# Host-transposed weights and a GpSimd time mix in a two-layer attention, expert and RWKV kernel

## The reference

```python
# first layer, experts
shared = silu(x @ sg_w.T) * (x @ su_w.T) @ sd_w.T
h = silu(einsum('th,eih->eti', x, eg_w)) * einsum('th,eih->eti', x, eu_w)
routed = einsum('eti,ehi,te->th', h, ed_w, comb)          # comb: routing factors
# second layer, each of 4 RWKV layers l
hx = time_shift(h)                                        # the token before
r = sigmoid((h * tmr + hx * (1 - tmr)) @ Wr.T)            # the receptance; k and v alike
x = x + (r * wkv(decay, first, k, v)) @ Wo.T
k2 = square(relu((h2 * cmk + hx2 * (1 - cmk)) @ Wck.T))
x = x + sigmoid((h2 * cmr + hx2 * (1 - cmr)) @ Wcr.T) * (k2 @ Wcv.T)
```

## Time and profile before

| | us |
|---|---|
| median of 3 runs | 1093.31 |
| lowest, highest | 1084.61, 1096.35 |
| the profiled execution | 1086.78 |
| its span (first to last instruction) | 1084.8 |
| PE busy in the span | 1020.1 (94%) |
| DVE busy | 768.1 (71%) |
| ACT busy | 582.5 (54%) |
| GpSimd busy | 63.6 (6%) |
| mean granted TensorE clock | 0.985 |

### The profile page before, as it was taken

The page is one execution under the profiler, slowest core; times in us unless marked ns, Lnnn a source line. Parts: engine busy times, 40 slices in busy tenths (PEclk is TensorE's granted clock), DMA queues, the critical chain, the costliest instruction groups (busy, mean ns, idle before and its releaser), DMA issues. The chain is left out here.

```text
span 1084.8 us, 12618 instructions
## 1 busy us (share of the span) xinstructions
PE 1020.1 (94%) x3858; PEld 445.8 (41%) x3858; DVE 768.1 (71%) x1332; ACT 582.5 (54%) x902; POOL 63.6 (6%) x152
## 2 busy tenths in 40 slices
PE   6889999999889999999999999879999999998998
PEld 3553444443333444444444443324344443443433
DVE  4879888888467555555555555588889988987575
ACT  4235666667774222222222222668789778875743
POOL 1011222222110000000000000000000000000000
PEclk9899999999999999999999999989999999999999
DMA  3732121200142544555545461100000020000001
GB/s 96 231 83 51 38 47 45 55 26 11 30 103 45 122 106 102 128 114 116 124 106 129 101 136 41 42 0 23 10 21 12 1 51 1 0 1 1 0 1 39
DMA packets 49980, 64.68 MB, mean 60 GB/s; under 512 B 17570, under 2 KB 41232, under 8 KB 45328
## 3 DMA queue, kind: packets, MB, share of 16 engines
q1 hardware_dynamic: 49100, 63.28, 25.1%
q10 hardware_dynamic: 832, 0.79, 0.2%
HBM read 55.87 MB, written 5.77 MB: 57 GB/s over the span
## 5 line engine op out<-in xcount | busy, mean ns | idle before, releaser
L977 ACT ACTIVATE pt<-psum 128x1024 f32<-128x1024 f32 (+1 forms) x192 | 150.2, 815 | 106.0 <-PE psum L748 105.6
L1131 DVE TENSOR_REDUCE part_max<-psum 128x1 f32<-128x512 f32 (+3 forms) x304 | 184.2, 658 | 31.9 <-PE psum L730 19.3
L1288 DVE TENSOR_TENSOR moe_gu<-moe_silu,psum 128x512 f32<-128x512 f32 x132 | 90.8, 688 | 150.4 <-PE psum L891 146.1
L1115 ACT ACTIVATE moe_silu<-psum 128x512 f32<-128x512 f32 x112 | 66.9, 598 | 200.0 <-PE psum L886 200.0
L891 PE MATMUL psum<-h,moe_wt 128*128 128x512 f32 x264 | 135.3, 594 | 1.5 <-DVE moe_gu L1288 1.5
L886 PE MATMUL psum<-h,moe_wt 128*128 128x512 f32 x264 | 134.9, 593 | 1.0 <-issue 1.0
L896 PE MATMUL psum<-moe_hid,moe_wt 128*128 128x512 f32 x264 | 135.0, 593 | 0.7 <-DVE moe_hid L1296 0.7
L726 PE MATMUL psum<-ka,qa 72*128 72x512 bf16 (+3 forms) x384 | 113.6, 337 | 4.5 <-DVE part_max L1131 1.6
L748 PE MATMUL psum<-qa,ka 75*128 75x512 bf16 (+3 forms) x384 | 93.8, 326 | 2.6 <-DMA qa<-neg_t 1.6
L1296 DVE TENSOR_TENSOR moe_hid<-moe_gu,qa 128x512 f32<-128x512 f32 x120 | 83.1, 692 | 13.6 <-DVE moe_gu L1288 5.8
L764 PE MATMUL psum<-pt,va_g 128*32 128x512 f32 (+3 forms) x768 | 81.8, 498 | 0.5 <-POOL pt L697 0.3
(11 more groups left out here) (274 smaller groups left out, 1362.3 us busy)
## 6 DMA issues: line engine op xcount, KB each, us to landing
qa<-comb_rows SPq DMA_DIRECT2D x56, 512.0 KB, 6.2
qa<-rows_q SPq DMA_DIRECT2D x21, 192.0 KB
ka<-rows_k SPq DMA_DIRECT2D x21, 192.0 KB
o_den<-acc SPq DMA_DIRECT2D x32, 64.0 KB, 2.1
moe_raw<-in_L_ffn_eg_w SPq DMA_DIRECT2D x32, 64.0 KB, 5.5
moe_raw<-in_L_ffn_eu_w SPq DMA_DIRECT2D x32, 64.0 KB, 5.3
moe_raw<-in_L_ffn_ed_w SPq DMA_DIRECT2D x32, 64.0 KB, 5.0
qa<-comb_rows SPq DMA_DIRECT2D x16, 128.0 KB, 3.2
```

Of the source, the lines that this page charges most:

```text
L977: act.activation(pt[:, u % 4, :, 0:n], score_bank[u % 2][:, :, 0:n], ACT.Exp, scale=SCALE)\
L1115: act.activation(sg[:, c % 2, :], g_bank[:, :], ACT.Silu).then_inc(silu_done, 1)
L1131: dve.tensor_reduce(part_max[:, h0:h0 + heads, slot], bank_of("fill", f)[:, 0:heads * nk].rearrange("p (h n) -> p h n", h=heads), AX_X, AL ...
L1288: dve.tensor_tensor(gu[:, at % 2, :], sg[:, at % 2, :], u_bank[:, :], ALU.mult).then_inc(gu_done, 1)
```

## The change

The host lays out three arrays, `moe_w`, `time_w` and `channel_w`, with the contraction dimension first. Then:

- The raw tiles of the expert weights, all `turn_weights` and `keep_weights` are gone. Loads go straight into the tiles that PE reads. The first five sets are loaded in one go during attention; after that, gate and up weights of step s + 2 are loaded into the tile of step s once its last `up` is done (`u_psum`), and the down weight once its last `down` is done (`y_psum`).
- In the RWKV stage `turn_a`, `turn_c` and `keep_c` are gone; the channel weights have two tiles by turns; the output weight is loaded in place; `keep_a` makes four scaled copies and one plain copy from SBUF in place of seven operations from PSUM.
- GpSimd makes `mix_r` = (here - before) * tmr + before, in three operations of 128x512 for each half unit, 48 in all. PE does one receptance product on it in place of two. `channel_scale` of DVE waits for GpSimd's mixing of the same unit, one body earlier.

```diff
-def load_experts(sp, G, A, s, k):
-    ...
+def load_expert(sp, A, s, tile, what, sem):
+
+    sp.dma_start(tile[:, what, :], A["moe_w"][bass.ds(s, 1), :, what, :].rearrange("o p j m -> p (o j) m")).then_inc(sem, 16)
...
                 with sp.Fori(PRE // 2, (STEPS - 3) // 2) as i:
                     for k in (1, 0):
                         s = 2 * i + 2 - k
-                        sp.wait_ge(w_turned, s + 1)
-                        load_experts(sp, G, A, s + 2, k)
+                        sp.wait_ge(u_psum, 4 * s + 4)
+                        load_expert(sp, A, s + 2, wt[k], slice(0, 2), gu_in[k])
                         sp.wait_ge(hid_done, 4 * s + 4)
                         factors(s + 2, factor[1 - k], slice(0, T), factor_in[1 - k])
+                        sp.wait_ge(y_psum, 4 * s + 4)
+                        load_expert(sp, A, s + 2, wt[k], slice(2, 3), down_in[k])
...
-                        if c == 1 and not last:
-                            turn_weights(s + 1, 1 - k)
+                        if c == 2:
+                            pe.wait_ge(down_in[k], 16 * loads)
...
+                for u in range(UNITS):
+                    for q in range(2):
+                        n = 2 * u + q
+                        pool.wait_ge(h_time, n + 1)
+                        if u:
+                            pool.wait_ge(r_psum, n - 1)
+                        pool.tensor_tensor(mix_r[:, q, :], here(u, q), before(u, q), ALU.subtract).then_inc(mix_step, 1)
+                        pool.wait_ge(mix_step, 2 * n + 1)
+                        pool.tensor_scalar(mix_r[:, q, :], mix_r[:, q, :], vec(TMK + 2, u), None, ALU.mult).then_inc(mix_step, 1)
+                        pool.wait_ge(mix_step, 2 * n + 2)
+                        pool.tensor_tensor(mix_r[:, q, :], mix_r[:, q, :], before(u, q), ALU.add).then_inc(mixed_p, 1)
...
                 def receptance(u, q):
                     if u == UNITS:
                         return
+                    pe.wait_ge(mixed_p, 2 * u + q + 1)
                     if u:
                         pe.wait_ge(G.ln.scaled, ln_channel(u - 1, q) + 1)
-                        shifted(G.bank[q], u, R_HERE, R_BEFORE, q).then_inc(r_psum, 1)
                     else:
                         pe.wait_ge(k_kept, q + 1)
-                        shifted(G.bank[4 + q], u, R_HERE, R_BEFORE, q).then_inc(r_psum, 1)
+                    pe.matmul((G.bank[q] if u else G.bank[4 + q])[:, :], wt_a[u // 2 % 2][:, R_HERE, :], mix_r[:, q, :],
+                              start=True, stop=True).then_inc(r_psum, 1)
...
                 def channel_scale(u, q):
+                    dve.wait_ge(mixed_p, 2 * u + 2)
                     ln_scale(dve, G, ln_channel(u, q), here(u, q), vec(LN2W, u), q)
```

More of the change, by code:

```diff
@@ L549, in stage_core @@
         factor_in = [mem.sem(f"moe_factor_in{k}") for k in range(2)]
-        w_turned, w_kept = mem.sem("moe_turned"), mem.sem("moe_kept")
+        first_w_in = mem.sem("moe_first_w")
+        gu_in, down_in = ([mem.sem(f"moe_{what}_in{k}") for k in range(2)] for what in ("gu", "down"))
         g_psum, u_psum, y_psum = mem.sem("moe_g"), mem.sem("moe_u"), mem.sem("moe_y")
@@ L1115, in step @@
                         act.activation(sg[:, c % 2, :], g_bank[:, :], ACT.Silu).then_inc(silu_done, 1)
-                        if c == 1 and not last:
-                            keep_weights(s + 1, nxt)
                 for g in range(NG):
@@ L1412, in stage_rwkv @@
         m = Memory(nc, ctx)
[L1413 to L1414 removed]
+        raw_a, a_in, c_in, wo_in = G.raw_a, G.a_in, G.c_in, mem.sem("rw_o_in")
+        wt_a, wt_c = ([m.sb(f"wt_{what}{k}", [P, n, P]) for k in range(2)] for what, n in (("a", 7), ("c", 9)))
         rest = m.sb("rest_tm", [P, 12])
@@ L1426, in stage_rwkv @@
         kvs = m.sb("kvs", [P, 2, CH])
-        a_turned, a_kept = mem.sem("rw_a_turned"), mem.sem("rw_a_kept")
-        c_turned, c_kept = ([mem.sem(f"rw_c_{what}{i}") for i in range(3)] for what in ("turned", "kept"))
+        a_kept = mem.sem("rw_a_kept")
+        mix_r, mix_step, mixed_p = m.sb("mix_r", [P, 2, CH]), mem.sem("rw_p_step"), mem.sem("rw_p_mixed")
         start = mem.sem("rw_start")
@@ L1850, in body @@
                     down(p, 0, 2)
-                    if u % 2 and u < LAST:
-                        turn_a(l + 1)
                     down(p, 1, 1)
@@ L2528, in build @@
         G.ln = LnSems(mem)
-        G.raw = [mem.sb(f"moe_raw{k}", [P, 3, P]) for k in range(2)]
-        G.raw_in = [mem.sem(f"moe_raw_in{k}") for k in range(2)]
         G.h = mem.sb("h", [P, T])
```

231 lines of the change are left out of this document (79 added, 152 removed).

## The result

The changed kernel takes 1078.86 us, the median of 19 runs (1077.01 to 1090.17); the kernel before took 1091.47 us in 19 runs beside it (1084.61 to 1104.27). The ratio is 0.9907 with a 95% interval of 0.9887 to 0.9927: 0.9% faster, about 10 us (the ratio is near that of the means, and the medians differ by 12.6). The forecast was 1082, in a range of 1072 to 1094.

The account below looks back on a forecast made before the run. PE was taken to bound the expert steps, ACT's chain the RWKV bodies; -10.0 + 0.3 - 0.9 - 0.5 + 1.6 + 0.7 + 0.5 = -8.3 us, put between 1078.5 and 1085.0 at 1082, range 1072 to 1094.

Parts of the forecast that it names:

- case A: Whole kernel: the forecast itself, experts pay and RWKV bodies don't, -8.3 us; chance 0.42.
- Expert weights: Expert steps: 33 turned sets at 0.32 us of PE each, sum -10.0 us, with +0.3 for loads not hidden.
- Start of the RWKV stage: Before unit 0's mod_var: the wait of 0.72 us for DVE's copies of turned weights goes, -0.9 us.
- Turning in the bodies: RWKV bodies: removing turn_c gives 0.12 us in each of four odd bodies, -0.5 us.
- What the product is worth: RWKV bodies' second part: of 1.72 us saved on PE, ACT lets through 0.15 (even) or 0.58 (odd).
- GpSimd's durations: GpSimd's mix: 1.12 us per two-input operation, 0.65 per one-input one, 3.2 us a half unit.
- DVE's lateness: RWKV bodies: DVE, waiting while GpSimd reads SBUF, is 1.4 us late, between 0 and 2.2.
- The slack: RWKV bodies: DVE's idle time before its two kvs absorbs 1.3 us of its delay.
- Unit 0: End of unit 0, where PE waits for DVE: half of DVE's 1.4 us delay added, +0.7 us.
- The clock: PE in the RWKV stage: products at half clock after more idle time, +0.5 us for one or two events.
- case E: RWKV stage: rival in which the clock falls in most bodies at 1.7 us each, +3, 1093 us; chance 0.10.
- Against the median: Starting point: 1078.5 us from the profiled run, 1085.0 from the median; the forecast put between, 1082.

Follow-up runs that it names:

- turn_back: The changed kernel with three 128-column products put back in each of the 27 looped expert steps, results unread; median 1091.13 us.
- no_mix: The changed kernel without GpSimd's mix, PE's one receptance product reading the normed tile and the receptance mixing left out; median 1077.58 us.
- late_free: The changed kernel with the second half unit's mix made late and PE doing both receptance products without waiting for it; median 1093.11 us.
- two_products: The changed kernel with GpSimd's mix taken out and both receptance products put back, host-laid weights kept; median 1077.36 us.
- e2b: Not a run: a buffer that DVE writes from gap and decay in the changed kernel's unit 0; that row takes 1.67 us.
- late_mix: The changed kernel with GpSimd starting the second half unit's mix only after DVE's channel mix of the unit before; median 1104.98 us.
- half_mix: The changed kernel with GpSimd mixing only each unit's first half unit, PE doing two receptance products on the second; median 1082.31 us.

## Why the prediction was right, and where it was not

The sum was -8.3 us against -7.9 between the two profiled executions, and case A, the experts pay and the RWKV bodies do not, is what happened. That the sums lie so near is luck in part: the RWKV stage was forecast at +1.4 and came at -0.1, and the start, forecast at 0, came at +2.3. Step by step:

- *Expert weights*: -9.7 forecast, -9.24 - 0.44 = -9.68 in the trace; turn_back gives 0.32 a step back. Only the -9.24 is shown (29 sets of 0.32 are 9.3): the stretch that holds the -0.44 moves by 5.7 us between profiles. Loads are hidden: no product of the steps between 395 and 660 us waits, and the 128 KB of gate and up weights land 2.0 us after their issue. The factors of steps 5 and 6 cost nothing that shows, where +0.3 was counted.
- *Start of the RWKV stage*: -0.9 forecast. `time_bias` of unit 0 starts 689.94 - 671.14 = 18.80 us after the stage's first product, before 698.29 - 678.53 = 19.76: -0.96.
- *Turning in the bodies*: 0.12 forecast for the first part, 0.13 measured (17.75 to 17.62).
- *What the product is worth*: the claim that ACT lets through next to nothing was right; no_mix has the number, 0.11 us a body where PE has neither turning nor second product. PE's idle time before the last down, said to be over 1 us, is 0.61, since 0.94 of waiting already stands at the fifth up.
- *GpSimd's durations*: wrong in one term. Subtraction 1.04 for 1.12 forecast, addition 1.09 to 1.50 for 1.12, but the multiplication by a vector takes 1.56 at the least where 0.65 was taken from a one-input operation of another kind. A half unit takes 3.9 and not 3.2, both end 14.8 us into an odd body (15.1 into an even one) and not 13.1. The lesson is in the choice: a row of another operation of the same engine is no bound for this one.
- *DVE's lateness*: 1.4 forecast for every body, 0.79 measured in an odd one and 1.19 in an even one. I let DVE wait for each whole GpSimd operation. The rows of the odd body show less: L2113 is not delayed at all (0.5 forecast), L2117 loses 0.37, the two L2121 lose 0.84. In the even body L2113 loses 0.11 and the two L2121 lose 1.0 (2.43). The Trainium skill, SBUF — State Buffer, Who interferes with whom, has DVE with two SBUF inputs contend with a GpSimd read, and this case agrees (rows above). The full block for a whole instruction, which the page states for DVE's two-port modes and which I took for all of these, gives my 1.4, and the trace does not show it: L2117 ends at 802.49 + 1.06 = 803.55 while GpSimd's multiplication still runs to 802.20 + 1.68 = 803.88, and both engines' rows grow at once, 3.41 for 1.56 and 2.98 for 2.29 below. The row that I leaned on had shown less already: a DVE operation standing still until GpSimd is done at 308.27 + 0.41 = 308.68 and then taking its 0.42 would have lasted 0.79, and it lasted 0.65.
- *The slack*: 1.3 forecast, 0.5 real (late_free), and the road over `mix_c` and the fifth up was not seen. Too much lateness against too much slack: the two errors cancelled, which was luck. Odd bodies came to -0.25 (forecast 0.0, which is +0.1 less the 0.12 of turning), even ones to +0.58 (forecast +0.4). From unit 2 on that is +1.11 in the trace, where these terms give 3 x 0.4 - 3 x 0.02 = +1.1.
- *Unit 0*: +0.7 forecast. DVE's row that PE waits for came 1.9 us later (PE's wait at the end of unit 0 is 7.23 us for 3.62), but units 0 and 1 together are only 0.7 longer than in two_products, because unit 1 is 1.2 shorter, at a granted clock of 0.77 for 0.68 in its first 13 us.
- *The clock* (E): no body shows a fall; 1.00 from unit 2 to the last, with waits of 0.69, 0.69, 0.94 and 0.61 in each. The 0.5 was not spent. In late_free, with longer waits, it happened in one body of five and cost 39.78 - 38.20 = 1.6 us, near the 1.7 that case E assumed.
- *Against the median*: going half way between profiled run and median gave 1082; the median came to 1078.9. The median of three runs that I started from, 1093.3, came down to 1091.5 with 19. Before's median lies 5 us over its profiled run, the changed kernel's on it.

## What to carry to other kernels

Before work is moved off a busy engine, measure what the engine behind it lets through: here two saved products of 0.86 us a body were worth 0.11 us, so a helper that makes a body 0.3 us longer had already lost. Of the three parts of this change, the mix on GpSimd is the one to leave out: two_products, with the new weight layout alone, is 3.3 us shorter in the RWKV stage. Work for GpSimd is best put where DVE is idle; half of this mix was free there, and the other half cost more than all of PE's saving brought. Removing work from an engine that never waits (27 expert steps) pays in full, and its price can be read from one distance between two starts.

## What the runs showed of the hardware that was not expected

- GpSimd multiplies 128x512 float32 by a per-partition vector in 1.56 us at the least, slower than it subtracts two such tiles (1.04).
- DVE and GpSimd slow each other while both read SBUF, and both can lose at once. In the changed kernel's unit 0 (DVE's scan and exponents; GpSimd's multiplication):

```profile
694.86 2.98 DVE L2128 TENSOR_TENSOR_SCAN pp<-decay,k_s 128x1024 f32<-128x1024 f32 x1 [2.95 <-ACT k_s L1868]
697.87 1.53 DVE L2135 TENSOR_TENSOR gap<-k_s,pp 128x1024 f32<-128x1024 f32 x1
699.43 1.67 DVE L2141 TENSOR_SCALAR e2b<-gap,decay 128x1024 f32<-128x1024 f32 x1
```

```profile
695.78 3.41 POOL L1512 TENSOR_SCALAR mix_r<-mix_r,vec 128x512 f32<-128x512 f32 x1
```

  The scan takes 2.29 alone, the two after it 1.22 and 0.75, and the multiplication 1.56. The third is a DVE operation with one SBUF input tile, and loses most in proportion; so does L2105 at 798.44 (0.89 for 0.49). In late_mix, against a DVE without pauses, GpSimd took 8.5 us for 3.7 and DVE lost 2.0.
- GpSimd's addition for the first half unit takes 1.09 us in odd units and 1.27 in even ones, with DVE idle for most of it. The reason is open. It was not the reason of the longer even bodies in half_mix. In the changed kernel the addition for the second half unit takes 1.50 in even units from unit 2 on and 1.32 in odd ones, and DVE is 1.19 late for 0.79. That fits the 0.3 by which even bodies are longer there, but no run takes the addition alone out.
- The clock ahead of the experts differs from run to run of the same program and goes with differences of up to 5.7 us (272.2 to 277.9 up to the first expert product; 0.97 for 1.00 between 100 and 275 us in two profiles of the changed kernel), half of what this change brings.
